# Attention: k's softmax shifted and summed inside four exponentials on ScalarE

## What is computed

```python
k = xn @ Wk + bk
k = jnp.where(mask, -jnp.inf, k)
q = jax.nn.softmax(q, axis=-1)      # over the 16 features of a head
k = jax.nn.softmax(k, axis=2)       # over the 64 steps of a sequence
attn = jnp.einsum('bhse,bhsd->bhed', k, v)
y = jnp.einsum('bhtd,bhed->bhte', q, attn)
```

## Time and profile before

| | |
|---|---|
| median of 3 runs | 2119.62 us (2118.67 to 2122.14) |
| span of the profiled execution, first to last instruction | 2117.5 us |
| attention stage (j = 0 to 70) | about 40 to 505 us |
| scan stage | from there to the end |

### The profile page before, as it was taken

The page is one execution under the profiler, slowest core; times in us unless marked ns, Lnnn a source line. Parts: engine busy times, 40 slices in busy tenths (PEclk is TensorE's granted clock), DMA queues, the critical chain, the costliest instruction groups (busy, mean ns, idle before and its releaser), DMA issues. The chain is left out here.

```text
span 2117.5 us, 43927 instructions
## 1 busy us (share of the span) xinstructions
PE 1944.8 (92%) x13241; PEld 1533.2 (72%) x13241; DVE 1903.4 (90%) x3692; ACT 1688.2 (80%) x3586; POOL 1480.2 (70%) x1754
## 2 busy tenths in 40 slices
PE   4999999995799999999999999999999999999860
PEld 2666666663478878787878878787887878787760
DVE  3999999994799999999999999999999999999973
ACT  1565565653899999999999999999999999999740
POOL 2688888886368678696968768696877869685420
PEclk9999999997999999999999999999999999999995
DMA  5122222211000000000000000000000000000408
GB/s 157 46 69 64 70 67 66 70 54 60 1 11 11 11 11 16 7 17 16 11 11 11 11 11 16 17 11 11 11 11 11 16 7 21 1 11 2 169 25 303
DMA packets 71548, 80.84 MB, mean 38 GB/s; under 512 B 12243, under 2 KB 63635, under 8 KB 69268
## 3 DMA queue, kind: packets, MB, share of 16 engines
q1 hardware_dynamic: 66132, 69.65, 10.3%
q10 hardware_dynamic: 5184, 8.39, 1.1%
HBM read 44.46 MB, written 33.55 MB: 37 GB/s over the span
## 5 line engine op out<-in xcount | busy, mean ns | idle before, releaser
L693 ACT ACTIVATE decay<-dtT,decay_rate 128x256 f32<-128x256 f32 x2048 | 863.7, 495 | 0.4
L574 PE MATMUL bank<-ident,decay 128*128 128x128 f32 x4096 | 617.7, 273 | 45.6 <-DVE state L827 20.7
L584 PEld LDWEIGHTS bank<-ident,scaled 128*128 128x128 f32 x4096 | 490.1, 142 | 213.3 <-issue 180.0
L584 PE MATMUL bank<-ident,scaled 128*128 128x128 f32 x4096 | 618.0, 274 | 0.2 <-POOL scaled L493 0.2
L574 PEld LDWEIGHTS bank<-ident,decay 128*128 128x128 f32 x4096 | 476.5, 141 | 61.7 <-ACT decay L693 51.6
L493 POOL TENSOR_SCALAR scaled<-state,bc 128x512 f32<-128x512 f32 x384 | 264.6, 697 | 209.8 <-DVE state L827 178.7
L493 POOL TENSOR_SCALAR scaled<-fresh,bc 128x512 f32<-128x512 f32 x384 | 265.3, 697 | 180.9 <-DVE fresh L827 122.7
L817 DVE TENSOR_TENSOR bank<-bank,fresh 128x512 f32<-128x512 f32 x512 | 340.0, 691 | 46.2 <-PE bank L574 42.5
L817 DVE TENSOR_TENSOR bank<-bank,state 128x512 f32<-128x512 f32 x512 | 343.6, 692 | 33.7 <-PE bank L574 30.4
L827 DVE SCALAR_TENSOR_TENSOR fresh<-dtx,bc,bank 128x512 f32<-128x512 f32 x512 | 357.1, 738 | 0.0
L827 DVE SCALAR_TENSOR_TENSOR state<-dtx,bc,bank 128x512 f32<-128x512 f32 x512 | 357.1, 738 | 0.0
(11 more groups left out here) (158 smaller groups left out, 3178.3 us busy)
## 6 DMA issues: line engine op xcount, KB each, us to landing
xt<-in_x_dram SPq DMA_DIRECT2D x64, 128.0 KB, 2.3
resid<-x SPq DMA_DIRECT2D x64, 128.0 KB, 1.7
normed<-xh SPq DMA_DIRECT2D x64, 128.0 KB, 1.7
ssm_out<-yo SPq DMA_DIRECT2D x32, 256.0 KB, 2.1
fin_r<-resid SPq DMA_DIRECT2D x8, 1024.0 KB, 12.5
xg<-normed SPq DMA_DIRECT2D x60, 128.0 KB, 2.1
mask_bc<-in_mask_BxS_ik_dram SPq DMA_DIRECT2D x64, 64.0 KB, 2.9
fin_y<-ssm_out SPq DMA_DIRECT2D x32, 128.0 KB, 2.9
```

The costliest lines, as they stand in the source:

```text
L574: mm = pe.transpose(dec_bank[i % DECAY_BANKS][:, m * P:(m + 1) * P], decay[:, i // BLOCK % 2, n % GROUP, m, t % HALF * P:(t % HALF + 1) * ...
L584: mm = pe.matmul(y_bank[t % HALF][:, m * P:(m + 1) * P], scaled[:, i % RING, m * P:(m + 1) * P], ident[:, :], is_transpose=True, start=Fal ...
L693: act.activation(decay[:, block % 2, e // CB, m, :], dtT[c % 2][:, m, half * HTOK:(half + 1) * HTOK], ACT.Exp, scale=decay_rate[:, m, n:n ...
```

## The change

The subtract (L1382) and the sum (L1335) on VectorE are dropped. The maximum is written negated (`kmax_neg`). ScalarE does an exponential for each of the 4 groups instead of one over all, with the negated maximum as its bias and its sum written to `ksum`, which now has two slots. The four exponentials wait for the maximum and for the free slot of ksum; the maximum waits until the previous tile's exponentials have read kmax_neg; the reciprocal of k moves ahead of the reciprocal of q.

```diff
@@ scalar @@
-                    later(act, S["k_shifted"], k)
-                    kk = kT[:, k % 2, :, :].rearrange("p a b -> p (a b)")
-                    act.activation(kk, kk, ACT.Exp).then_inc(S["k_exp"], 1)
+                    later(act, S["k_max"], k)
+                    reuse(act, S["k_rec"], k, 2)
+                    for g in range(FB * SEQS):
+                        kk = kT[:, k % 2, g, :]
+                        ins = act.activation(kk, kk, ACT.Exp, bias=kmax_neg[:, g:g + 1],
+                                             accum_out=ksum[:, k % 2, g:g + 1])
+                    ins.then_inc(S["k_exp"], 1)
@@ vector @@
                     later(ve, S["k_exp"], k3)
-                    reuse(ve, S["k_rec"], k3, 1)
-                    ve.tensor_reduce(ksum[:, :], kT[:, k3 % 2, :, :], AX.X, ALU.add).then_inc(S["k_sum"], 1)
+                    reuse(ve, S["k_normed"], k3, 1)
+                    ve.reciprocal(krec[:, :], ksum[:, k3 % 2, :]).then_inc(S["k_rec"], 1)
                     later(ve, S["q_sum"], k3)
                     ve.reciprocal(qrec[:, k3 % 4, :], qsum[:, :]).then_inc(S["q_rec"], 1)
-                    later(ve, S["k_sum"], k3)
-                    reuse(ve, S["k_normed"], k3, 1)
-                    ve.reciprocal(krec[:, :], ksum[:, :]).then_inc(S["k_rec"], 1)
...
                     later(ve, S["k_biased"], k2)
-                    ve.tensor_reduce(kmax[:, :], kk, AX.X, ALU.max).then_inc(S["k_max"], 1)
+                    reuse(ve, S["k_exp"], k2, 1)
+                    ve.tensor_reduce(kmax_neg[:, :], kk, AX.X, ALU.max, negate=True).then_inc(S["k_max"], 1)
...
-                    later(ve, S["k_max"], k2)
-                    ve.tensor_tensor(kk, kk, kmax[:, :, None].to_broadcast([P, FB * SEQS, STEPS]), ALU.subtract)\
-                        .then_inc(S["k_shifted"], 1)
```

More of the change, by code:

```diff
@@ L134, in build @@
         kT = sb("kT", [P, 2, FB * SEQS, STEPS], attn_mem)
-        kmax = sb("kmax", [P, FB * SEQS], attn_mem)
-        ksum = sb("ksum", [P, FB * SEQS], attn_mem)
+        kmax_neg = sb("kmax_neg", [P, FB * SEQS], attn_mem)
+        ksum = sb("ksum", [P, 2, FB * SEQS], attn_mem)
         krec = sb("krec", [P, FB * SEQS], attn_mem)
@@ L197, in build @@
         names = ("x_stats x_meanvar x_rstd x_norm xT_ready xnT_ready qv_ready kT_ready mneg_ready "
-                 "k_biased k_max k_shifted k_exp k_sum k_rec k_normed q_max q_shifted q_exp q_sum q_rec v_ready "
+                 "k_biased k_max k_exp k_rec k_normed q_max q_shifted q_exp q_sum q_rec v_ready "
                  "kq_turned kq_ready at_half at_ready at_masked y_ready y_scaled y_stats y_meanvar y_rstd y_norm ynT_ready "
```

## The result

The changed kernel takes 2144.06 us (median of 4, 2141.75 to 2148.01) against 2119.32 before: 1.0107 of the time before, 95% interval 1.009 to 1.0125. The forecast was 2142. The profiled execution spans 2140.0 us, 22.5 more than before; the sum had 22.5.

The account below looks back on a forecast made before the run. VectorE was taken to end last, TensorE right behind, in a loop through ScalarE: 5.95 + X, X from 0.98 to 1.36, 7.31 us per iteration. Span 2117.5 plus 22.5 is 2140.0, plus 2.1 to device time: 2142 us, range 2126 to 2174.

Parts of the forecast that it names:

- the sum: Forecast total over the attention stage: +22.4 for 59 iterations, +1.8 early turns, -1.7 at the end, +22.5 us in all.
- X: ScalarE's time from xnT leaving to kq's start: 0.98 before, forecast 1.36 us, in a loop of 5.95 + X.
- The mechanism: Attention loop through TensorE and ScalarE's kq sets the iteration: four exponentials with sums delay kq, 6.94 to 7.31 us.
- The steady part: The 59 steady intervals of the attention stage, each forecast 0.38 us longer: +22.4 us.
- The rest: Pipeline's first two full turns, +1.8 us, and its end, up to -1.7 us: forecast to cancel to +0.1.
- Rival D: TensorE idles 0.7 of 7.3 us, losing full clock for part of the attention stage: 2160 or more; chance 0.03.
- The stated span of 2130 to 2159 us: Forecast time with the exponential's slot at 0.24 to 0.27 and each sum at 0.06 to 0.15 us.
- Rivals A: On ScalarE the sums are free, leaving inside the activation: X 0.96 to 1.0, 2119 to 2121 us; chance 0.10.
- C: On ScalarE each sum waits for its exponential: X 2.12, 2187 us; half of that, 2166; chance 0.17 for both.
- Rival B: VectorE was the bound and lightening it pays, TensorE recovering at most 0.34 per iteration: 2099 us; chance 0.05.

Follow-up runs that it names:

- the kernel with eight pieces: The changed kernel with eight exponentials of 32 columns, each with its sum, instead of four of 64 columns: 2288.81 us, ratio 1.0782.

## Why the prediction was right

Step by step, against the profile of the changed kernel:

| Step | Forecast | Measured |
|---|---|---|
| slot of a 64-column exponential with a bias column | 0.24 | 0.24 (329.86 - 329.62) |
| a sum | 0.10, a step of its own | 0.09 (329.95 - 329.86), a step of its own |
| first exponential to kq (X) | 1.36 | 1.32 |
| L1115 to L1150; to xnT; kq to L1115 | 4.18; 0.41; 0.63 | 4.19; 0.42; 0.64 |
| xnT to the first exponential | 0.73 | 0.70 |
| one iteration | 7.31 | 7.27 |
| 59 iterations | +22.4 | +19.3 |
| TensorE's wait at L1115 | 0.7 | 0.70 |
| VectorE's idle time per iteration | about 1.0 | 0.80 |
| VectorE's busy time | -53 | -31.8 |

*The mechanism* held, and the experiments tie each part of it to a run. That VectorE's relief buys nothing in the changed kernel: 0.67 us of spare work changed no steady iteration. That X counts one for one: 6.90, 7.27 and 8.38 us per iteration at X = 0.96, 1.32 and 2.43 (5.94 to 5.95 is left over each time). That it is a matter of place and not of load: kq put first.

*The sum was right to the microsecond in part by luck.* The steady part was 3.1 too high: the slots of 0.10 and 0.73 were 0.09 and 0.70. The rest was forecast at +0.1 and came to +3.2: the maximum of iteration 5 starts at 66.4 us in place of 63.45 (+2.9, forecast +1.8), and all that follows the steady stretch adds 0.3 more (forecast -1.7). VectorE's lead did give something back at the end: TensorE's longest wait for attnT fell from 1.70 to 1.09 us, and from the last xnT to the last fth it is 25.6 us in place of 26.5. But from there to the scan's first L693 it is 59.7 in place of 58.7. That part ranges from 58.4 to 59.9 over all profiled executions, and its cause stays open. In the filling the third turn took 8.90 us where 6.38 + 0.9 = 7.3 was forecast. The other 1.6 us fit a clock that fell: 4 us at a mean of 0.59 lose 4 x 0.41 = 1.6 (an estimate). In the changed kernel's profile, from 52 to 60 us:

```profile
52.00:56.00 4.00, 2.08 (x14) 1.84 (x15) 1.55 (x6) 2.57 (x12) 1.65 (x4) 0.99 0.21 53
56.00:60.00 4.00, 4.00 (x10) 1.84 (x8) 2.24 (x8) 0.00 (x0) 0.94 (x2) 0.59 0.07 16
```

Rival D, a clock that falls because TensorE idles more, was given a chance of 0.03 and told against by a window at full clock with TensorE busy 2.75 of 4 us. In the steady iterations that was right. In the filling it was a small true part of the loss: just before the fall TensorE was busy 2.08 of 4 us where the kernel before had 2.75, so the window in the earlier trace rows was not the one that the changed kernel would show. In the kernel with eight pieces the clock is about half of the loss.

*The stated span of 2130 to 2159 us* for the forecast's own terms leaves out the 2.1 us from span to device time that the forecast has; with them it is 2132 to 2161. Nothing else hangs on it.

*VectorE's busy time* was forecast from durations, 64 times two of 0.41. But neighbours overlap by 0.07 to 0.09, so each removed operation took only its slot out of the busy time: 64 x 0.67 = 43. The rest fits the two new gaps per iteration, at which the overlap with the neighbour is lost: 64 x 2 x 0.08 = 10 (an estimate), which leaves 33. By the same token VectorE is idle 0.80 in place of 7.27 - 6.27 = 1.0. It didn't touch the time.

*Rivals A and C* were told apart by the trace itself: 256 entries of 193 ns on ScalarE (not free), each starting 0.24 after its exponential and not after its end at 0.34 (no drain). *Rival B* fell with the spare work, and yet names the potential rightly: once kq stands ahead, the same relief is worth some 0.6% (1.0002 without it, 0.9942 with it), down to TensorE's own 6.76 us; its estimate of 0.34 per iteration was too much, 6.94 - 6.76 = 0.18 is there.

## What to carry to other kernels

When engines hand work round in a loop, add up one turn of it, start to start, and put the change into that sum before looking at busy shares; an engine with 40% to give can still be the one that everybody waits for. Splitting an operation into pieces costs the fixed part of each piece, at the place in the queue where it stands: look at who waits behind it, and move the awaited instruction ahead first. A relief of one engine can cost time and a reordering of another measure nothing, and the two together still give a gain; so try a reordering again after each change of the work.

## What the runs showed of the hardware that was not expected

- A sum written by an activation is a separate entry on ScalarE, 186 to 198 ns long; the next instruction begins 0.09 us after the entry's start. It overlaps both neighbours; four of them cost 0.37 us per iteration.
- In the kernel with eight pieces TensorE waited 1.55 us for kq in an iteration of 8.4 us, and its granted clock then fell to 0.50; over 440 us the mean was 0.86. In the changed kernel it waited 0.43 (matmuls) to 0.67 (weight loads) in 7.27 us, and in no steady iteration did the clock fall. A wait lengthened by 1.1 us thus cost 1.1 us plus, on the average of all iterations, about as much again through the clock.
- The clock during the filling of the pipeline differs between executions of one kernel: a third turn of 8.90 and of 11.21 us, 2.3 of the 5.9 us between these two profiled spans. Over all profiled executions the third turn is 5.95 to 6.38 us where the granted clock from 56 to 60 us was 1.00 (the kernel before, with and without kq first, and both of the changed kernel with kq first), and 8.55 to 11.8 us in the eight where it was 0.50 to 0.59. What decides which it is stays open.
